# Re-ordering the SyncE transfer queue of a two-layer cross-attention kernel, and one VectorE reciprocal with it

## The reference, cut to what matters

```
# layer 0, 8 heads of 40; enc = first 73 context rows, ca = last 4
hs      = mha(x @ Wq, enc @ Wk, enc @ Wv)
ca_q1   = (ca^T @ Wq_ca)[:, indices]                 # 192 channels spread to 256 rows
ca_hs1  = mha(ca_q1, x, x)                           # "channel" attention, keys and values are x
ca_hs2  = mha(ca_hs1 @ Wq, ca @ Wk_ca, ca @ Wv_ca)
x1      = (hs + ca_hs2) @ Wout + b_out + x
# layer 1, 20 heads of 16
out     = mha(x1 @ Wq1, ctx @ Wk1, ctx @ Wv1) @ Wo + bo + x1
```

## Time and profile before

| | us |
|---|---|
| median of 3 runs | 401.69 (400.5 to 403.73) |
| profiled execution, its own time | 401.35 |
| span of that execution, first to last instruction | 399.6 |
| PE busy | 338.0 (85% of the span) |
| DVE, ACT, POOL busy | 195.3, 161.3, 114.1 |
| mean granted TensorE clock | 0.897 of full speed |
| DMA | 61.51 MB in 53543 packets, 154 GB/s |

### The profile page before, as it was taken

How to read it: one execution, slowest core, us unless ns; L and a number is a source line. 1 busy time by engine, 2 the same in 40 slices (tenths; PEclk the granted TensorE clock), 3 DMA queues, 4 the chain that set the end, 5 groups by cost and what they waited for, 6 DMA issues and landing times.

```text
span 399.6 us, 7714 instructions
## 1 busy us (share of the span) xinstructions
PE 338.0 (85%) x2988; PEld 261.3 (65%) x2988; DVE 195.3 (49%) x421; ACT 161.3 (40%) x343; POOL 114.1 (29%) x118
## 2 busy tenths in 40 slices
PE   4998869999899998999899899979996977967305
PEld 2777565787667776877686678758874854764205
DVE  5561135727716883485358527834692362271111
ACT  3540643164428423663446264526452615205000
POOL 5835220341035115411531252134111201211001
PEclk9996999999759998998999999988998986598756
DMA  8998837522753676766666766776585253131140
GB/s 246 294 341 246 213 98 235 102 68 95 228 121 103 165 239 155 130 178 212 152 140 201 206 151 130 225 169 146 115 257 136 77 115 125 28 60 65 37 112 39
DMA packets 53543, 61.51 MB, mean 154 GB/s; under 512 B 18164, under 2 KB 45268, under 8 KB 53508
## 3 DMA queue, kind: packets, MB, share of 16 engines
q1 hardware_dynamic: 53508, 61.03, 57.3%
HBM read 38.22 MB, written 22.40 MB: 152 GB/s over the span
## 4 chain that ended last, share of the span: by engine, by line
PE 37%; DMA 26%; SPq 12%; DVE 10%; ACT 9%; issue 5%; DVEq 0%; ACTq 0%
DMA den<-u 6%; DMA atu<-u_scratch 4%; DMA u_scratch<-u 4%; ACT prob L732 3%; SPq L339 3%; DVE negm L839 3%; PE bank L602 3%; DMA q_scratch<-q 3%; DMA denc<-uc 3%; PE bank L678 2%; PE bank L592 2%; PE bank L464 2%; PE bank L434 2%; PE bank L642 2%; DVE negmc L839 2%
## 5 line engine op out<-in xcount | busy, mean ns | idle before, releaser
L839 DVE TENSOR_REDUCE negm<-bank 128x5 f32<-128x385 f32 (+2 forms) x88 | 42.5, 552 | 14.3 <-PE bank L712 14.3
L732 ACT ACTIVATE prob<-bank 77x512 f32<-77x512 f32 (+1 forms) x96 | 41.1, 530 | 19.0 <-PE bank L509 18.9
L1069 POOL TENSOR_TENSOR at0lo<-atu,at0hi 120x512 fp32r<-120x512 f32 x8 | 10.1, 1266 | 96.3 <-ACT at0hi L722 96.3
L1063 POOL TENSOR_TENSOR at1lo<-atu,at1hi 128x512 fp32r<-128x512 f32 x8 | 10.2, 1269 | 92.9 <-DVE at1hi L905 92.9
L801 ACT ACTIVATE prob<-bank 73x512 f32<-73x512 f32 x32 | 16.3, 592 | 46.9 <-PE bank L660 46.9
L507 PE MATMUL bank<-q,kp 32*77 32x256 f32 x320 | 27.9, 431 | 6.1 <-ACT prob L732 3.8
L434 PE MATMUL bank<-at1hi,wo1hi 128*128 128x256 f32 (+1 forms) x48 | 16.0, 334 | 19.0 <-issue 18.0
L839 DVE TENSOR_REDUCE negmc<-bank 128x2 f32<-128x512 f32 x48 | 29.4, 681 | 3.0 <-PE bank L519 2.9
L722 ACT ACTIVATE q<-bank 120x512 fp32r<-120x512 f32 (+3 forms) x32 | 15.7, 490 | 29.7 <-PE bank L438 29.4
L990 DVE TENSOR_TENSOR u<-u,rb 128x1280 f32<-128x1280 f32 x8 | 15.2, 1899 | 24.6 <-DMA rb<-rec_scratch 24.6
L642 PE MATMUL bank<-at0hi,wo 120*128 120x256 f32 x48 | 18.0, 376 | 9.8 <-issue 9.8
(11 more groups left out here) (152 smaller groups left out, 871.5 us busy)
## 6 DMA issues: line engine op xcount, KB each, us to landing
q_scratch<-q SPq DMA_DIRECT2D x24, 360.0 KB, 5.3
q0s<-q_scratch SPq DMA_DIRECT2D x8, 960.0 KB
xkeys<-in_xkeys SPq DMA_DIRECT2D x8, 512.0 KB, 3.4
u_scratch<-u SPq DMA_DIRECT2D x8, 512.0 KB, 3.5
xt<-in_xt SPq DMA_DIRECT2D x8, 384.0 KB, 4.9
rb<-rec_scratch SPq DMA_DIRECT2D x16, 192.0 KB, 3.7
out_t<-x SPq DMA_DIRECT2D x8, 384.0 KB, 2.4
rb<-rec_scratch SPq DMA_DIRECT2D x32, 80.0 KB, 3.1
```

Of the source, the lines that this page charges most:

```text
L732: nc.scalar.activation(p1[:, h:h + n, :].rearrange("p h q -> p (h q)"), ps_of("SC1", j, d)[0:KEYS1, 0:n * SQ], ACT.Exp, scale=SCALE1)\
L839: return nc.vector.tensor_reduce(out=out, in_=in_, axis=AX, op=ALU.max, negate=True)
```

## The change

SP's loop is re-ordered, and one DVE instruction moves. On SP: (1) the store of the normalised layer-0 product now stands right behind the store of the channel reciprocals, and the three query stores behind it; the `rbc` loads come after those. (2) The `atu` loads of layer 0 follow `rbc`. (3) The `wo0` rows, formerly second in the pass, are loaded behind the stacked queries. (4) The channel keys, formerly loaded for the next batch at the end of a pass, are loaded for this pass's batch, behind the maxima rows and ahead of `den1`; the first batch's load at the start stays. (5) The gather of the channel denominators moves ahead of the wait for the `u1` stores and the three `atu` loads behind it. (In pass 0 the set-up load of k0s moves by one place, which changes nothing there.) On DVE: (6) the reciprocal of layer 1's denominators, with its wait, moves from ahead of the x1 additions to behind them. No transfer and no instruction is added or dropped.

```diff
                     sp.wait_ge(recc_ready, c + 1)
                     sp.dma_start(rc_d.rearrange("e n -> (e n)").rearrange("(p n) -> p n", p=128), recc[:, :]).then_inc(recc_st, 16)
-                    if c == 0:
-                        sp.wait_ge(v2w_st, 32)
-                    sp.dma_start(wo0[96:128, :, 2, :].bitcast(f32), v_d[c]).then_inc(v2w_in, 16)
+                    sp.wait_ge(u0_ready, c + 1)
+                    sp.dma_start(u0_d.rearrange("o r j q -> (o r) j q"), u0[:, :, :]).then_inc(u0_st, 16)
+                if s1:
+                    drained(sp, "Q", b, 0, 1)
+                    for v, part in enumerate((q0hi, q0lo, q0hi)):
+                        sp.dma_start(q_d[:, :, v].rearrange("g r q -> r g q"), part.bitcast(f32)).then_inc(q_st, 16)
+                if s2:
                     sp.wait_ge(recc_st, 16 * (c + 1))
                     for odd in range(2):
                         sp.dma_start(rbc[64 * odd:64 * odd + 48, :, :].rearrange("p a c -> p (a c)"),
                                      rc_d[odd].unsqueeze(0).to_broadcast([48, PAIRS * CAD])).then_inc(rbc_in, 16)
-                    sp.wait_ge(u0_ready, c + 1)
-                    sp.dma_start(u0_d.rearrange("o r j q -> (o r) j q"), u0[:, :, :]).then_inc(u0_st, 16)
-                if s1:
-                    drained(sp, "Q", b, 0, 1)
-                    for v, part in enumerate((q0hi, q0lo, q0hi)):
-                        sp.dma_start(q_d[:, :, v].rearrange("g r q -> r g q"), part.bitcast(f32)).then_inc(q_st, 16)
...
                 if s1:
                     sp.wait_ge(q_st, 48 * (b + 1))
                     sp.dma_start(q0s[0:120, :, :].bitcast(f32), ...).then_inc(q0s_in, 16)
+                if s2:
+                    if c == 0:
+                        sp.wait_ge(v2w_st, 32)
+                    sp.dma_start(wo0[96:128, :, 2, :].bitcast(f32), v_d[c]).then_inc(v2w_in, 16)
...
                 if s1:
                     place_maxima()
+                    if b:
+                        load_xkeys(b)
...
+                if s1:
+                    drained(sp, "CU", b, 0, 1)
+                    sp.dma_start(denc[:, :], uc[D0:128:64, :, :]).then_inc(denc_in, 16)
                 if s3:
                     sp.wait_ge(u1_st, 64 * (d + 1))
...
-                if s1:
-                    drained(sp, "CU", b, 0, 1)
-                    sp.dma_start(denc[:, :], uc[D0:128:64, :, :]).then_inc(denc_in, 16)
-                    if b + 1 < B:
-                        load_xkeys(b + 1)
... (DVE)
-                if s3:
-                    dve.wait_ge(den1_in, 16 * (d + 1))
-                    nc.vector.reciprocal(rec1[:, :], den1[:, :]).then_inc(rec1_ready, 1)
                 if s2:
                     ...
                         tt(x1[c % 3][:, m, :], ps_of("O", m, c)[:, 0:SQ], xt[c % 2][:, m, :], ALU.add)
                         tt(x1hi[:, m, :], ps_of("O", m, c)[:, 0:SQ], xt[c % 2][:, m, :], ALU.add).then_inc(free_of("O", m, c), 1)
+                if s3:
+                    dve.wait_ge(den1_in, 16 * (d + 1))
+                    nc.vector.reciprocal(rec1[:, :], den1[:, :]).then_inc(rec1_ready, 1)
```

More of the change, by code:

```diff
@@ L339, in _ @@
                         sp.dma_start(q_d[:, :, v].rearrange("g r q -> r g q"), part.bitcast(f32)).then_inc(q_st, 16)
[L340 to L343, removed]
                 if s2:
+                    sp.wait_ge(recc_st, 16 * (c + 1))
+                    for odd in range(2):
+                        sp.dma_start(rbc[64 * odd:64 * odd + 48, :, :].rearrange("p a c -> p (a c)"),
+                                     rc_d[odd].unsqueeze(0).to_broadcast([48, PAIRS * CAD])).then_inc(rbc_in, 16)
                     sp.wait_ge(u0_st, 16 * (c + 1))
@@ L350, in _ @@
                     sp.dma_start(atu[0:80, 2, :], u0_d[:, 0:D0, 3, :].rearrange("o r q -> r o q")).then_inc(at0u_in, 16)
+                if i == 0:
+                    sp.wait_ge(dve_init, 1)
+                    sp.wait_ge(k_st, 48)
+                    load_k0s(0)
                 if s1:
```

## The result

The changed kernel takes 437.24 us (433.8 to 439.62), the kernel before, on the same chip, 402.71: a ratio of 1.087 [1.074, 1.100]. The forecast was 416, in a range of 402 to 425. The direction was right, the size forecast less than half of it: 15.5 us summed, 34.5 measured. Executions over 1.5% longer than the fastest of their kernel are left out of the ratios in this text, while medians and ranges hold them all.

What follows compares the result with a forecast made beforehand. PE's order was taken to bound the kernel, with SP's transfer queue setting O's start. Terms 2.1 + 3.7 + 2.3 + 5.0 + 2.4 = 15.5 on 401.35 gave about 417, stated as 416, range 402 to 425.

Steps and rivals of the forecast that it cites:

- Clock: PE's lower speed costs 41 us; new waits ahead of S2 replace shorter ones ahead of O: +-4, taken as 0.
- Edits 1 and 2, `rbc`: `rbc` lands 8.0 us after `u0_ready`, `hsc` 3.8 later: +2.1 in pass 1, +3.7 in pass 2, +2.3 in passes 3 to 7.
- Rival 1: `rbc` overtakes query stores and lands 2.4 us later, not 3.8: 409, or 405 with half of edit 6 hidden; chance 0.16.
- `hsc`'s waits: Sign in the DVE trace: `hsc` would wait for `rbc` 3 to 5 us in every pass.
- V1's stretch: Pass 1: V1's products on PE, from the sixth, wait for the first SM bank: about +2.1 us.
- 2.1 + 3.7 + 2.3: Forecast delays in us from later `rbc`: pass 1, pass 2, and passes 3 to 7 net.
- A tie: nothing taken: `wo0` rows land 15.5 us after `u0_ready`, just as O could start: 0, up to +1 a pass.
- rival 3: O waits 1 to 2 us a pass for `wo0` rows: 422 to 427; chance 0.09.
- Edit 6: Later `rec1` delays `rec0`, the SM1 maxima and M1: +5.0 us over six passes, +2.4 in pass 8.
- Edits 4 and 5: Channel keys behind the maxima rows cost nothing; earlier channel denominators credited 0.4 us a pass from pass 4 on.
- Faster: Waits ahead of O go, if `rbc` lands within 6.7 us of `u0_ready`: 394; chance 0.08.
- Hardly matters: The order hardly matters, all terms at their lower ends: 402; chance 0.07.

Runs made afterwards that it cites:

- experiment 4: Changed kernel plus 14 to 40 idle matmuls a pass on PE ahead of S2, passes 2 to 8: 420.96 us, 1.040.
- experiment 11: Kernel before plus idle matmuls in PE's waits of over 0.4 us, ahead of O, S2 and M1: 399.41 us, 0.989.
- experiment 13: Changed kernel with edit 6 undone and idle matmuls on PE ahead of S2: 410.55 us, 1.021.
- experiment 5: Changed kernel with edits 1 and 3 undone, `rbc` and `wo0` rows both first again: 408.26 us, 1.014.
- experiment 8: Kernel before with edits 4 and 5, and `u0` stored first, then `rbc`, `wo0` rows, queries; `rec1` as before: 408.88 us, 1.017.
- 14: Kernel before with edits 4 and 5 alone: 0.995 from two of eleven executions; median of all 408.44 us.

## Why the prediction was right in direction and wrong in size

- **Clock: the step that failed.** "New waits ahead of S2 replace shorter ones ahead of O; a tenth more or less of the 41 us that this costs is +-4, taken as 0." It was 16.3 us by experiment 4; the kernel before gives back 4 in the same way (experiment 11), so that some 12 are the change's. PE's extra busy time points the same way: 15.7 us in passes 3 to 7. The prediction counted a new wait of 2 to 5 us as 2 to 5 us, in exchange for shorter ones ahead of O, without costing the half-speed work behind it. The Trainium skill, "TensorE: Matmul & The Clock Gate", section "HAM oscillation — how this bites in real kernels", describes the like: bursts of matmuls between waits for transfers start cold each time. The traces agree: 0.61 behind the wait of 2.46 us in pass 5, and 0.87 with idle matmuls in its place.
- **Edits 1 and 2, `rbc`: the mechanism right, the size a little small.** Rival 1, overtaking, fell: `rbc` landed behind all queries in every pass that has them. The Trainium skill's sentence on completion order ("DMA: Bandwidth & Descriptors", section "Queues, rings and completion order") did not help `rbc` here; the four transfers ahead of it landed in the order of their issue. Against `u0_ready`, `hsc` was 4.1 to 5.6 us later than before, where 3.8 was taken and 4.8 the upper end. `hsc`'s waits are as foreseen. V1's stretch came true in the profiled execution by the clock, not by the bank. Take off edit 6 and the clock (experiment 13), and 410.55 - 401.91 = 8.6 us are left, against 2.1 + 3.7 + 2.3 = 8.1; that these agree is luck, since there O is held by the `wo0` rows, which the prediction put at nothing. (The kernel before gains 4 from idle matmuls too, so against one filled alike it is some 11.)
- **Edit 3, "A tie: nothing taken": wrong, but hidden.** In the changed kernel O waits for the rows in one pass of seven, 1.9 us. But alone the edit costs 27 us. In passes 2 to 7 the rows landed 16.1 to 17.1 us after `u0_ready`, not 15.5; it did not show because PE, late and at half speed, came to O only 16.9 to 20.7 us after it. With the clock kept up, O waits for the rows in passes 2 to 7 (experiment 13), which is the mechanism of rival 3, "heavier". Taken apart, edits 1 and 3 cost 32 and 27 us, and undoing edit 1 alone gives back nothing.
- **Edit 6: mis-sized.** 7.4 forecast, 12.1 measured. `rec1` was put 4.9 us after O's start in pass 5 (234.2 - 229.35) and came 6.9 after it (256.54 - 249.65): the additions stand behind O, and O ran at half speed. From there on the reckoning held: `rec0` started 9.0 us after `rec1`'s end (9.1). Over passes 3 to 7, undoing the edit takes 9.8 us off (216.2 to 206.5, from O to O), and 5.2 off the end (95.2 to 90.0), while the stretch ahead was 3.2 longer in that execution. M1 was to wait for the maxima over six passes; it waits at most 0.15 us in passes 3 to 7, and longer only in the end. What was not foreseen is that SM1's matmuls wait 3.6 us for a bank that ACT drains (`uc`, L713), which is gone with `rec1` back in its place. The price also depends on the rest: edits 4, 5 and 6 together cost only 6 us (experiment 5).
- **Edits 4 and 5: no great error shown.** Edit 5 is worth about 4 us alone, 0.4 a pass was credited; edit 4's zero is neither refuted nor, by the waits of experiments 8 and 14, safe: with `rec1` ahead of the additions it makes CT wait. (The prediction's "8 KB of `den1`" are 20; nothing hangs on it.)
- **The other rivals.** "Faster" needed `rbc` within 6.7 us of `u0_ready`; it took 8.2 or more. "Hardly matters" fell with the result.

With some 12 us for the clock and 4.7 more for edit 6, the sum of 15.5 becomes some 32 of the 34.5 measured.

## What to carry to other kernels

When an edit puts a new wait of a few microseconds in front of TensorE, cost it twice: the wait, and the matmuls behind it at half speed; a few idle matmuls in the wait's place measure the second part without touching the first, as long as no other wait takes its place. When two transfers that one consumer needs are both moved back, undoing one of them can show nothing: undo both, and try each alone on the kernel before, or one of two nearly equal waits looks free. Moving a small instruction behind a batch of others moves every store and load that waits for it, and it inherits any slowdown of what it now stands behind.

## What the hardware showed that was not expected

A wait of 0.76 us, with two waits of 0.16 behind it, was followed by 6 us at a granted clock of 0.50 (experiment 8, pass 5). In the kernel before, the same place waits at most 0.2, and the clock from 233 to 247 is 1.00. It does not follow each time: in pass 3 of the same execution a wait of 0.78 us with two of 0.16 was followed by ten at 1.00, and in the changed kernel the clock fell behind S2's wait of 1.78 us in pass 7 and not behind the one of 1.80 in pass 3.

Raising the clock from 0.856 to 0.929 gave 16 us in the changed kernel, from 0.897 to 0.935 only 4 in the kernel before. That PE sets the pace in the one and not in the other is the likely reason, but it is not shown.

The 96 KB of `wo0` rows took 2.9 us from issue to landing (median) in the trace before, 7.8 behind the 960 KB of the stacked queries: in these runs the small transfer paid for the large one ahead of it on the queue.
